# Graph attention and a GNN layer on one core: mirror blocks of the exponentials by transposing packed 32-bit words

## What is computed

```
def attention(x, adj, beta):
    norm2 = jnp.linalg.norm(x, axis=1, keepdims=True)
    cos = beta[0] * (x @ x.T) / (norm2 @ norm2.T + 1e-07)
    masked = cos + (1.0 - adj) * -1000000000.0
    P = jax.nn.softmax(masked, axis=1)
    return P @ x

def neighbours(h, adj, W_self, W_neigh):
    deg = jnp.clip(jnp.sum(adj, axis=1, keepdims=True), 1.0)
    h_neigh = adj @ h / deg
    return h @ W_self + h_neigh @ W_neigh

h = jnp.maximum(_layernorm(x, axis=-1), 0.0)
x = x + attention(h, adj, beta)
h = jnp.maximum(_layernorm(x, axis=-1), 0.0)
x = x + neighbours(h, adj, W_self, W_neigh)
```

## Time and profile before

| | |
|---|---|
| median of 3 runs | 533.44 us (531.8 to 533.96) |
| the profiled execution | 531.57 us, span 529.8 us |
| mean granted TensorE clock | 0.987 |

### The profile page before, as it was taken

The page is one execution under the profiler, slowest core; times in us unless marked ns, Lnnn a source line. Parts: engine busy times, 40 slices in busy tenths (PEclk is TensorE's granted clock), DMA queues, the critical chain, the costliest instruction groups (busy, mean ns, idle before and its releaser), DMA issues.

```text
span 529.8 us, 12739 instructions
## 1 busy us (share of the span) xinstructions
PE 491.7 (93%) x5280; PEld 378.5 (71%) x5280; DVE 405.3 (76%) x700; ACT 340.3 (64%) x357; POOL 338.4 (64%) x382
## 2 busy tenths in 40 slices
PE   0178999999999999999999999999979999999996
PEld 0146777777777777777777777777768988889895
DVE  6989877999999999999999999999955123231253
ACT  2959876888798888788788878889971111101111
POOL 3889999877997997998898899798751000000000
PEclk9979999999999999999999999999998999999998
DMA  8034457555575666657556557566300000000001
GB/s 251 26 113 166 161 161 230 172 197 157 174 234 171 222 185 215 186 182 231 170 189 208 191 172 236 177 216 193 97 4 1 21 21 1 21 21 21 22 1 41
DMA packets 43710, 72.29 MB, mean 136 GB/s; under 512 B 2432, under 2 KB 10880, under 8 KB 43648
## 3 DMA queue, kind: packets, MB, share of 16 engines
q1 hardware_dynamic: 43648, 71.44, 43.2%
HBM read 69.34 MB, written 2.10 MB: 135 GB/s over the span
## 4 chain that ended last, share of the span: by engine, by line
PE 80%; POOL 8%; DVE 6%; issue 4%; DMA 1%; ACT 0%; SPq 0%; DVEq 0%; POOLq 0%
PE ps L933 21%; PE ps L860 10%; PE ps L875 9%; PE ps L862 9%; PE ps L843 9%; PE ps L845 9%; PE ps L844 9%; POOL adjm L355 2%; POOL adj_t L357 2%; PE ps L920 2%; PE ps L909 2%; DVE adj_t L548 1%; DVE adj_t L579 1%; DMA x_sb<-in_x_dram 1%; POOL table L310 1%
## 5 line engine op out<-in xcount | busy, mean ns | idle before, releaser
L497 ACT ACTIVATE e_hi<-ps,small 128x1024 f16<-128x1024 f32 x128 | 154.1, 1204 | 57.1 <-DVE ps L707 55.5
L707 DVE SCALAR_TENSOR_TENSOR ps<-adjm,small,ps 128x1024 f32<-128x1024 fp8e4 x128 | 164.2, 1283 | 16.7 <-POOL adjm L355 13.3
L715 DVE TENSOR_TENSOR e_lo<-ps,e_hi 128x1024 f16<-128x1024 f32 x128 | 156.0, 1218 | 2.1 <-ACT ps L498 1.5
L498 ACT ACTIVATE ps<-ps,small 128x1024 f32<-128x1024 f32 x128 | 149.7, 1169 | 0.0
L355 POOL TENSOR_SCALAR adjm<-stage 128x1024 uint8<-128x1024 f32 x128 | 133.7, 1045 | 17.0 <-DMA stage<-in_adj_dram 6.6
L357 POOL TENSOR_SCALAR adj_t<-stage 128x1024 uint8<-128x1024 f32 x128 | 133.8, 1045 | 10.2
L860 PE MATMUL ps<-table,e_hi 128*128 128x129 f16 x1024 | 131.8, 221 | 0.4
L862 PE MATMUL ps<-table,e_hi 128*128 128x128 f16 x1024 | 131.6, 218 | 0.0
L933 PE MATMUL ps<-table,adj_t 128*128 128x257 f16 x1024 | 118.7, 276 | 2.8 <-POOL table L379 2.8
L933 PEld LDWEIGHTS ps<-table,adj_t 128*128 128x128 fp8e4 x1024 | 99.9, 99 | 17.1 <-POOL table L379 3.1
L860 PEld LDWEIGHTS ps<-table,e_hi 128*128 128x128 f16 x1024 | 99.0, 97 | 18.2 <-issue 2.8
(11 more groups left out here) (90 smaller groups left out, 273.0 us busy)
## 6 DMA issues: line engine op xcount, KB each, us to landing
stage<-in_adj_dram SPq DMA_DIRECT2D x128, 512.0 KB, 4.3
x_sb<-in_x_dram SPq DMA_DIRECT2D x4, 512.0 KB, 6.2
out_dram<-x_sb SPq DMA_DIRECT2D x7, 256.0 KB, 2.3
out_dram<-x_sb SPq DMA_DIRECT2D x1, 192.0 KB, 2.1
stage<-in_L_gnn_W_neigh_dram SPq DMA_DIRECT2D x1, 64.0 KB, 1.8
stage<-in_L_gnn_W_self_dram SPq DMA_DIRECT2D x1, 64.0 KB, 1.9
out_dram<-x_sb SPq DMA_DIRECT2D x1, 64.0 KB, 1.5
small<-in_L_gnn_beta_dram SPq DMA_DIRECT2D x1, 0.5 KB, 2.8
```

The lines of the kernel that those rows point to most:

```text
L497: act.activation(ring(e_hi, n), scored(n), ACT.Exp, bias=exp_bias, scale=exp_scale).then_inc(s_ehi, 1)
L498: act.activation(scored(n), scored(n), ACT.Exp, bias=exp_bias, scale=exp_scale).then_inc(s_exp, 1)
L707: dve.scalar_tensor_tensor(scored(n), ring(adjm1, n), mask_scale, scored(n), ALU.mult, ALU.add).then_inc(s_masked, 1)
L715: dve.tensor_tensor(ring(e_lo, n), scored(n), ring(e_hi, n), ALU.subtract).then_inc(s_elo, 1)
```

## The change

Only the pairs on and above the diagonal blocks are computed. A pair is now (s, p, far): step s, pair of tiles p, and far is true where the 256 rows j lie above the step's 512 rows i. There are 72 pairs, 56 of them far, 16 near alone. In step 0 the pairs run 0 to 15; in each later step the far ones come first, then the two of the diagonal.

For each pair the exponentials are made unmasked, in chunks of 512 columns. ScalarE writes the float16 high half into the upper half of a 32-bit word (stride of two float16), VectorE the low half into the lower one (`low_part`). GpSimd multiplies the words, taken as float32, with the 8-bit adjacency (`mask_near`: the value stored for one is the bit pattern of 1.0). For a far pair TensorE also transposes the 8 blocks of 128x128 words (`turn`), and VectorE multiplies the result with the adjacency of the mirrored block (`mask_far`). Both go through 24 products (`attend_near`, `attend_far`), whose stationary operand is now every second float16 of a buffer. The near sums stay in PSUM over a step; the far sums of a pair (two tiles of rows) are added into SBUF, where x was (`spill`), so x is loaded once more (`load_x_again`). Word, near and far buffers have rings of two; the transposed words have one place (banks 3 and 4), the far sums one bank, the scores three banks of one chunk.

GpSimd converts the near tile of the adjacency (`convert`, L380), ScalarE the far one (L509); the mask of before (L355) is gone. The second h and the table of it are made during the attention. Of the last two row groups that work comes behind the last pair, and TensorE takes row tiles 0 to 7 of group 1 ahead of tiles 28 to 31 of group 0. The host packs the adjacency in the order of use.

```diff
-                dve.scalar_tensor_tensor(scored(n), ring(adjm1, n), mask_scale, scored(n), ALU.mult, ALU.add
-                                         ).then_inc(s_masked, 1)
...
-                    act.activation(ring(e_hi, n), scored(n), ACT.Exp, bias=exp_bias, scale=exp_scale).then_inc(s_ehi, 1)
-                    act.activation(scored(n), scored(n), ACT.Exp, bias=exp_bias, scale=exp_scale).then_inc(s_exp, 1)
+                for c in range(2):
...
+                    act.wait_ge(s_scores, 2 * k + c + 1)
+                    act.activation(half(word16, k, c, 0, HIGH, TPS), score(k, c), ACT.Exp, bias=exp_bias, scale=exp_scale)
+                    act.activation(score(k, c), score(k, c), ACT.Exp, bias=exp_bias, scale=exp_scale).then_inc(s_exp, 1)
...
-                dve.tensor_tensor(ring(e_lo, n), scored(n), ring(e_hi, n), ALU.subtract).then_inc(s_elo, 1)
+                dve.tensor_tensor(half(word16, k, c, 0, LOW, TPS), score(k, c), half(word16, k, c, 0, HIGH, TPS), ALU.subtract
+                                  ).then_inc(s_elo, 1)
...
+            def mask_near(k):
+
+                pool.wait_ge(s_elo, 2 * (k + 1))
+                pool.wait_ge(s_adjd, k + 1)
+                if k >= 2:
+                    pool.wait_ge(s_pvd, k - 1)
+                pool.tensor_tensor(ring(near, k), ring(word, k), adj_t[:, near_adj(k)], ALU.mult).then_inc(s_near, 1)
...
+            def turn(k, c, t):
+
+                m = FAR_BEFORE[k]
+                if c == 0 and t == 0 and m >= 1:
+                    pe.wait_ge(s_far, m)
+                if t == 0:
+                    pe.wait_ge(s_elo, 2 * k + c + 1)
+                ins = pe.transpose(turned(k, c)[:, t * P:(t + 1) * P], ring(word, k, c, 1)[:, t * P:(t + 1) * P], ident)
...
+            def scores_and_turns(k, n):
+
+                new, flip = k < NP, n < NP and PAIR[n][2]
+                for i in range(8):
+                    if new and i < 6:
+                        score_product(k, i // 3, i % 3)
+                    if flip:
+                        turn(n, i // TPS, i % TPS)
...
+            def mask_far(k):
+
+                m = FAR_BEFORE[k]
+                dve.wait_ge(s_turn, m + 1)
+                dve.wait_ge(s_adjt, m + 1)
+                if m >= 2:
+                    dve.wait_ge(s_pvt, m - 1)
+                dve.tensor_tensor(
+                    ring(far, m).rearrange("p (c t n) -> p c t n", c=2, t=TPS),
+                    ps[:, TURN:TURN + 2, :].rearrange("p c (t n) -> p c t n", t=TPS),
+                    far_adj(k, adj_t).rearrange("p t (c n) -> p c t n", c=2), ALU.mult).then_inc(s_far, 1)
...
-            pe.wait_ge(s_ulo, 2)
-            scores(0)
-            pe.wait_ge(s_ulo, 4)
-            scores(1)
-            pe.wait_ge(s_ulo, 6)
-            scores(2)
             pe.wait_ge(s_ulo, NS)
             pe.wait_ge(s_first, 5)
-            for n in range(NP):
-                if n + RING < NP:
-                    scores(n + RING)
...
-                attend(n)
+            scores_and_turns(0, NP)
+            scores_and_turns(1, NP)
+            for k in range(NP):
+                scores_and_turns(k + 2, k + 1)
+                if PAIR[k][2]:
+                    attend_far(k)
+                attend_near(k)
+                if k == 10:
+                    mean_products()
...
+                for k in range(NP):
+                    s, at = PAIR[k][0], k - FIRST[PAIR[k][0]]
+                    if s >= 1 and at == 0:
+                        evacuate(s - 1)
+                    if k + 1 < NP and PAIR[k + 1][2]:
+                        mask_far(k + 1)
+                    if k + 2 < NP:
+                        words(k + 2, general)
+                    if PAIR[k][2]:
+                        spill(k)
...
+                    if s >= 1 and at == 0:
+                        new_rows(s - 1)
```

More of the change, by code:

```diff
@@ L860, in attend @@
-                        pe.matmul(acc(t), part, tab(2 * pair + c, D, TW), start=first and c == 0 and t % 2 == 0, stop=False,
+                        rows = s * TPS + t
+                        high, low = half(far16, m, c, t, HIGH), half(far16, m, c, t, LOW)
+                        pe.matmul(far_acc(c), high, tab(rows, D, TW), start=c == 0 and t == 0, stop=False,
                                   skip_group_check=True)
-                        last = pe.matmul(acc(t, 0, D), part, tab(2 * pair + c, 0, D), start=False, stop=False,
+                        pe.matmul(far_acc(c, 0, D), high, tab(rows, 0, D), start=False, stop=False, skip_group_check=True)
@@ L863, in attend @@
+                        last = pe.matmul(far_acc(c), low, tab(rows, D, TW), start=False, stop=t == TPS - 1,
                                          skip_group_check=True)
[L864 to L870 removed]
@@ L872, in attend @@
                 for c in range(2):
                     for t in range(TPS):
-                        part = e_lo[:, n % RING * TILE + c * ROWS + t * P:n % RING * TILE + c * ROWS + (t + 1) * P]
-                        last = pe.matmul(acc(t), part, tab(2 * pair + c, D, TW), start=False, stop=end and c == 1,
-                                         skip_group_check=True)
-                last.then_inc(s_pvlo, 1)
+                        rows = 2 * p + c
+                        high, low = half(near16, k, c, t, HIGH), half(near16, k, c, t, LOW)
@@ new lines, in attend_near @@
+                        pe.matmul(acc(s, t), high, tab(rows, D, TW), start=first and c == 0 and t % 2 == 0, stop=False,
+                                  skip_group_check=True)
+                        pe.matmul(acc(s, t, 0, D), high, tab(rows, 0, D), start=False, stop=False, skip_group_check=True)
+                        last = pe.matmul(acc(s, t), low, tab(rows, D, TW), start=False, stop=end and c == 1,
+                                         skip_group_check=True)
+                last.then_inc(s_pvd, 1)
@@ L1007, in _, with pair_order, packed @@
             multiply_parts(g, 1, [3])
+def pair_order(n):
+    steps, pairs = n // 512, n // 256
+    order = [(s, p, p // 2 > s) for s in range(steps)
+             for p in ([*range(pairs)] if s == 0 else [*range(2 * s + 2, pairs), 2 * s, 2 * s + 1])]
+    return order, steps, pairs
+def packed(adj):
+    import numpy as _np
+    n = adj.shape[0]
+    order, steps, pairs = pair_order(n)
+    flipped = adj.T
+    near = flipped.reshape(pairs, 2, 128, steps, 512)
+    far = flipped.reshape(steps, 4, 128, pairs, 256)
+    tiles = []
+    for s, p, both in order:
+        tiles.append(near[p, :, :, s, :].transpose(1, 0, 2).reshape(128, 1024))
+        if both:
+            tiles.append(far[s, :, :, p, :].transpose(1, 0, 2).reshape(128, 1024))
+    return _np.stack(tiles)
 _INS = ["x", "adj", "L0_gnn_beta", "L1_gnn_W_self", "L1_gnn_W_neigh"]
```

714 lines of the change are left out of this document (390 added, 324 removed).

## The result

The changed kernel takes 536.73 us (median of 10 runs, 533.84 to 541.17), the kernel before took 532.69 beside it (10 runs, 530.64 to 533.98). The ratio is 1.0088, with an interval of 1.0054 to 1.0123: slower by 0.9%. 514 had been forecast; the time lies in the range, the direction was wrong.

The account below looks back on a forecast made before the run. TensorE was taken as the bound, VectorE close behind. 13.8 us gained in the attention and 4.9 behind it, 18.7 off the profiled 531.57, give 512.9; with 1.9 for the median it forecast 514, range 490 to 545.

Parts of the forecast that it names:

- The stream: TensorE's work in the attention: 56 far pairs of 4.93 us and 16 near of 2.67, together 318.8 us.
- hidden: Rival: transposes' weight loads run behind products of scores in TensorE's stream, 18 us less, 496 us; chance 0.08.
- dearer transposes: Rival: each change of type in TensorE's stream makes transposes cost more, 18 us more, 532 us; chance 0.09.
- strided loads: Rival: weight loads of every second float16 set the pace of 3072 products, 160 us more, 674 us; chance 0.12.
- The clock and the transposes: Rival: TensorE's clock falls in the attention because transposes don't count as activity, 830 us; chance 0.02.
- Clock 1.00 through the attention: Sign that the prediction is right: TensorE at full clock through the whole attention; a clock under 1 would show it wrong.
- The other engines per pair: Per far pair ScalarE under 3.9 us, VectorE 3.1, GpSimd 3.3, all within 4.93; GpSimd alone named as exceeding near pairs' 2.67.
- The first two pairs: Start of the attention: each chunk passes ScalarE and VectorE before the ring turns, 2.2 us of stalls.
- Five steps' starts: VectorE's queue with new rows, about 3 us, delays `low_part` at steps' starts; 0.6 us of stall each, 3 in all.
- The last steps: Attention's end, few far pairs: GpSimd falls behind TensorE's 2.67 us near pairs; three stalls, 7 us in sum.
- The start: Before the attention: GpSimd's conversions delay the chain by 1.7 us; first `attend` at about 44.7 instead of 43.07.
- GpSimd or another engine that a pair outruns: Rival: `mask_near` over 3.9 us makes GpSimd the bound; at 4.5 us, 590 us in all; chance 0.07.

Follow-up runs that it names:

- e7: Changed kernel with one of a far pair's eight transposes, from the second far pair on; 514.84 us in one run.
- e1: Changed kernel with GpSimd's `mask_near` multiplying 16 of 1024 columns, every wait kept; 521.79 us in one run.
- e5: Changed kernel with the row work of steps 1 to 6 in three pieces, each between `mask_far` and `low_part`; 528.44 us, 0.9937 of the kernel before.
- e6: Changed kernel with row-work pieces between `mask_far` and `low_part`, first conversions behind inverse norms, scores not awaiting all low halves; 522.96 us, 0.9822 of the kernel before.
- e2: Changed kernel with ScalarE's first exponential written densely instead of into every second float16; 534.9 us in one run.
- e3: Changed kernel with the row work of steps 1 to 6 in three pieces, each behind a `spill`; 542.68 us, 1.0234 of the kernel before.

## Why the prediction was wrong

The attention ended at 399.38 us instead of 373.5. These 25.9 us are all of the error against the profiled span: the part behind it gained 4.9 us, as forecast (before 529.8 - 387.26 = 142.5, now 537.0 - 399.38 = 137.6).

- **The stream** of 318.8 us was right: 4.93 and 2.67 us a pair, transposes at 0.11 (timeline, e7), strided weight loads at 98 to 101 ns. The rivals of hidden, of dearer transposes and of strided loads fell by this.
- **The clock and the transposes**: 1.00 from 105 to 130 us with eight transposes a pair, so that rival fell too. By what the Trainium skill says in "TensorE: Matmul & The Clock Gate", Part 4, that transposes don't count as activity for the clock, it could have fallen there; the rows do not agree. It fell in the start and behind stalls. "Clock 1.00 through the attention" failed for that reason.
- **The other engines per pair**: GpSimd 2.01 + 1.05 = 3.06 (3.3 forecast) and VectorE 3.1 (L776 1.22, L758 two of 0.735, L791 0.41) were right. ScalarE was put too low: 2 x (0.937 + 0.741) + 1.07 = 4.4 us by durations, some 3.9 from start to start, where 2.4 to 2.7 and a conversion were "under 3.9". It still fits into 4.93. It does not fit into the 2.67 of a near pair, for which the prediction named only GpSimd; where two near pairs follow each other at a step's end, ScalarE is the one that is late (below).
- **The first two pairs**: 1.5 + 0.6 us of stalls, 2.2 forecast.
- **"Five steps' starts"** is the step that failed. "The new rows of eleven small instructions, about 3" take 5.2 us, and instead of 0.6 a step the stalls are 15.0 us in sum (five of 2.24, four of 0.61, three of 0.46) where 3 stood. The mechanism put there, VectorE's queue in front of `low_part`, was right; the row work in it was charged at the price of instructions that wait for nobody. Without the wait for `mask_near` the stall is 0.57 with all the row work in one place (e1), and e5 takes 1.6 of each 2.24 away by place alone. The cause stood in the rows that the prediction used for the start: eight VectorE instructions of 128 columns took 4.56 us beside GpSimd and 1.75 without. That 2.6-fold price was applied to one stage of the start and to no other.
- **The last steps**: 9.3 us (1.59, 3.03, 1.46, 3.23) where 7 stood.
- **Half clock behind stalls**, at most half of 20.4 us, 10.2, was not in the sum at all. It is what is left: the attention took 352.5 us instead of 328.8, 23.7 more; 14.2 are stalls (26.4 against 12.2), 9.5 remain.
- **The start**: the first near product at 46.88 instead of 44.7. The delay was 2.6 us instead of 1.7, and behind the first score 8.8 us passed instead of 7.5.

- **The last line of the sum**: 512.9 and the 1.9 above it are 514.8, not 514. Nothing hangs on it.

Of the rivals none came true as it was put. On the slower side stood strided weight loads, GpSimd or another engine that a pair outruns, and a clock lowered by transposes. All three are costs of every pair; the loss came from a queue at the steps' starts, on an engine busy for 60% of the span, and from a clock that fell behind stalls.

The two stalls that stay at most steps' ends in e5 and e6 can be read from VectorE's timeline of the changed kernel:

```profile
190.90 0.73 DVE L758 TENSOR_TENSOR word<-ps,word 128x512 f16<-128x512 f32 x1 [1.54 <-ACT ps L533]
...
194.03 1.22 DVE L776 TENSOR_TENSOR far<-ps,adj_t 128x1024 f32<-128x1024 f32 x1 [0.96 <-PE ps L926]
195.18 0.72 DVE L758 TENSOR_TENSOR word<-ps,word 128x512 f16<-128x512 f32 x1
```

The one of 0.46 ends with the first of these lines, a `low_part` that waits for ScalarE, which is busy there without a gap; e2, with shorter exponentials, takes 0.1 to 0.2 off it, and 0.55 off the one of 1.59, where the second h stands in ScalarE's stream too. The one of 0.61 is a chain: the last transpose of a pair starts at 193.51, then come `mask_far` and the first half of `low_part`, and the next transpose starts at 196.04. Between the two TensorE has only the 24 products of a near pair instead of 48. No run took this chain apart, and e2 and e5 leave it at 0.61. What stays open is why the clock fell behind two of the five stalls of 2.24 and not behind the other three.

## What to carry to other kernels

When a change moves operands of VectorE's short instructions from PSUM into SBUF, or work onto GpSimd, charge those instructions with the rest of the GpSimd instruction that runs beside them: L710 waited out most of one of 2.01 us for 0.17 us of work. Short instructions suffer most, and it matters where they stand: the same pieces cost 2.8 us of stalls at a step's start in e3 and 0.6 in e5. Where the trace of before has one kind of instruction at two durations, find out what runs beside it before taking either. And when a bound engine is relieved, the stalls that its work had covered come out (e7: 42 us of work removed, 22 gained); behind some of them the clock falls too.

## What the runs showed of the hardware

- A VectorE TENSOR_SCALAR of 3 or 4 columns, SBUF to SBUF, took 1.73 to 1.90 us where `mask_near` had just begun and ended with it, 0.17 where no GpSimd instruction ran beside it; an addition of 128 columns with one input in PSUM kept its 344 ns beside GpSimd (kernel before); reciprocal and batch statistics of like size kept their 0.18 and 0.22 us a piece beside the same instruction.
- A float32 transpose cost 0.11 us between products of 512 float16 columns, as in a run of its own.
- Weight loads with a stride of two float16 took as long as dense ones, 98 to 101 ns.
- Writing an exponential of 512 columns with a stride of two float16 took 937 ns, dense 780.
- Stalls of 2.2 us and more were followed four times by 3.4 us at 1.2 GHz and three times not. The ten executions of the changed kernel differ in this: 533.84 us at a mean clock of 0.985, 541.17 at 0.968.
